# Two banks per maximum in a chain of three attention layers: pairs of banks, one bank for late projections, reciprocals by way of DRAM

## The reference

```python
# layer 0: 8 heads of 16; a bilinear position bias is added per query and per key
attn = einsum('bhdi,bhdj->bhij', q * scale, k) + pos[..., :, None] + pos[..., None, :]
y = w_proj(softmax(attn) @ v) + b_proj
out = layer_norm_over_channels(x + y)
# layers 1 and 2: 8 heads of 32
xn = group_norm(x);  q, k, v = linear(xn)
out = w_o(softmax(q k^T / sqrt(32)) v) + b_o + residual
# layer 3: a small gated attention with rank 32, without heads, at the end
```

## Time and profile before

| | |
|---|---|
| median of the timed runs | 482.24 us |
| profiled execution, its own time | 485.04 us |
| span of that execution | 483.3 us |
| TensorE busy | 453.1 us (94%), 2210 matmuls |
| VectorE busy | 362.8 us (75%) |
| ScalarE busy | 263.4 us (54%) |
| GpSimd busy | 214.4 us (44%) |
| mean granted TensorE clock | 0.968 |

### The profile page before, as it was taken

How to read it: one execution, slowest core, us unless ns; L and a number is a source line. 1 busy time by engine, 2 the same in 40 slices (tenths; PEclk the granted TensorE clock), 3 DMA queues, 4 the chain that set the end, 5 groups by cost and what they waited for, 6 DMA issues and landing times.

```text
span 483.3 us, 7009 instructions
## 1 busy us (share of the span) xinstructions
PE 453.1 (94%) x2210; PEld 239.1 (49%) x2210; DVE 362.8 (75%) x748; ACT 263.4 (54%) x515; POOL 214.4 (44%) x195
## 2 busy tenths in 40 slices
PE   8989999999896999999999799989999999979996
PEld 6544445553266575445444233657544544423463
DVE  7699888884777599987878356669997787817673
ACT  3238777775703237776757462224786677745032
POOL 8300031238010007897979811002799898960100
PEclk9979999999896999999999889999999999989999
DMA  5330544103300264679853520045388953551002
GB/s 154 56 64 21 156 69 125 22 8 62 61 6 1 60 147 100 154 155 195 189 105 57 104 48 21 1 109 126 72 176 166 191 102 70 98 100 26 0 1 87
DMA packets 20368, 41.87 MB, mean 87 GB/s; under 512 B 7170, under 2 KB 8458, under 8 KB 20076
## 3 DMA queue, kind: packets, MB, share of 16 engines
q1 hardware_dynamic: 15036, 25.41, 22.3%
q0 software_dynamic: 5152, 16.00, 17.9%
q10 hardware_dynamic: 144, 0.02, 0.0%
HBM read 5.94 MB, written 1.05 MB: 14 GB/s over the span
## 4 chain that ended last, share of the span: by engine, by line
PE 64%; DVE 10%; POOL 10%; DMA 4%; issue 4%; SPq 3%; ACT 3%; ACTq 0%; POOLq 0%; DVEq 0%
PE PV L1016 14%; PE S L977 13%; PE S L1005 13%; POOL SUMS L523 9%; DVE max L732 6%; DMA SUMS<-SUMS 3%; PE PV L929 3%; PE S L1140 3%; PE M L1029 3%; SPq L338 2%; PE PV L955 2%; PE S L1174 2%; PE M L955 2%; PE S L955 1%; SPq L331 1%
## 5 line engine op out<-in xcount | busy, mean ns | idle before, releaser
L732 DVE TENSOR_REDUCE max<-S 128x1 f32<-128x512 f32 x384 | 239.3, 683 | 39.7 <-PE S L977 38.7
L587 ACT ACTIVATE E<-S 128x512 f32<-128x512 f32 x384 | 206.5, 609 | 58.9 <-PE S L1005 53.3
L523 POOL TENSOR_TENSOR SUMS<-E 128x512 f32<-128x512 f32 x120 | 158.4, 1449 | 106.4 <-ACT E L587 102.0
L977 PE MATMUL S<-k_stack,q_stack 126*128 126x512 f32 x384 | 171.2, 460 | 5.8 <-DMA k_stack<-kL 3.4
L1005 PE MATMUL S<-q_stack,k_stack 128*128 128x512 f32 x384 | 156.0, 418 | 5.7 <-ACT E L587 5.2
L977 PEld LDWEIGHTS S<-k_stack,q_stack 126*128 126x128 f32 x384 | 72.9, 191 | 64.7 <-DVE max L732 35.4
L1005 PEld LDWEIGHTS S<-q_stack,k_stack 128*128 128x128 f32 x384 | 73.3, 193 | 38.3 <-ACT E L587 22.0
L1016 PE MATMUL PV<-E,V 128*32 128x512 f32 x768 | 92.0, 599 | 0.0
L1016 PEld LDWEIGHTS PV<-E,V 128*32 128x32 f32 x768 | 20.7, 110 | 46.9 <-issue 26.0
L498 POOL TENSOR_TENSOR att<-pv_sb,rec_sb 128x512 f32<-128x512 f32 x9 | 12.4, 1378 | 63.0 <-DMA rec_sb<-den_sb 63.0
L576 ACT ACTIVATE mHL<-S 8x128 fp32r<-8x128 f32 x48 | 12.7, 264 | 50.2 <-PE S L995 50.2
(11 more groups left out here) (175 smaller groups left out, 342.2 us busy)
## 6 DMA issues: line engine op xcount, KB each, us to landing
SUMS<-SUMS POOLq DMA_DIRECT2D x30, 512.0 KB, 5.7
k_stack<-kH SPq DMA_DIRECT2D x28, 128.0 KB, 2.3
q_stack<-qH SPq DMA_DIRECT2D x40, 64.0 KB, 2.0
rec_sb<-den_sb SPq DMA_DIRECT2D x9, 256.0 KB
q_stack<-qH SPq DMA_DIRECT2D x16, 128.0 KB, 2.8
k_stack<-kL SPq DMA_DIRECT2D x14, 128.0 KB, 4.1
k_stack<-kH SPq DMA_DIRECT2D x22, 64.0 KB, 2.3
q_stack<-qL SPq DMA_DIRECT2D x20, 64.0 KB, 2.0
```

The source lines that it names most:

```text
L523: pool.tensor_tensor(SUMS[:, slot, :], E[:, E_PLAN[s][0], :], E[:, E_PLAN[s + 1][0], :], ALU.add).then_inc(sum_ready, 1)
L587: act.activation(E[:, slot, :], B[:, ring_of_scores(s) % B_RING, :], ACT.Exp, scale=1.0 if l == 0 else float(HEAD_DIM[l]) ** -0.5).then_in ...
L732: dve.tensor_reduce(max8[:, m % 2, 2 * t + half:2 * t + half + 1], A[:, n % A_RING, :], AX.X, ALU.max).then_inc(a_used, 1)
L977: pe.matmul(A[:, n % A_RING, :], q_stack[0:SHIFT_ROW, slot, q0:q0 + P], k_stack[0:SHIFT_ROW, slot, k0:k0 + HALF], start=True, stop=True).t ...
```

## The change

- Ring A has four banks, used as two pairs. TensorE writes two banks and then signals once; VectorE takes the maxima of both in one reduce (output two elements, input 2 x 512) and signals once. TensorE waits before an even product for the pair before the last one. The seventh bank, which was M, is the fourth bank of ring A during the steps.
- Late projections all go through PV; each waits for the reader of the one directly before it. Their steps are stretched: -15 to 3 as before, then 8, 10, 14, 16, 21, 23, with new steps for ScalarE and VectorE. The second v projection of layer 0 goes through PV too.
- The denominators of blocks 0 and 1 take a slot of ring B; those of block 2 and of the last block still use M, after all maxima of the layer are read. ScalarE copies those of blocks 0 and 1 at the steps 49 and 81 in place of 54 and 86.
- The reciprocals are written to DRAM as 128 rows of 16, and spread from there to `rec_sb`.

```diff
-A_RING = 3
+A_RING = 4
-        S = ctx.enter_context(nc.psum_tensor("S", [P, 6, HALF], F32))
-        A = S[:, 0:A_RING, :]
-        B = S[:, A_RING:A_RING + B_RING, :]
-        PV = ctx.enter_context(nc.psum_tensor("PV", [P, HALF], F32))
-        M = ctx.enter_context(nc.psum_tensor("M", [P, HALF], F32))
+        banks = ctx.enter_context(nc.psum_tensor("banks", [P, 8, HALF], F32))
+        S, M, PV = banks[:, 0:6, :], banks[:, 6, :], banks[:, 7, :]
+        B = banks[:, 0:B_RING, :]
+        A = banks[:, B_RING:B_RING + A_RING, :]
...
-        LATE_PE = [{}] + 2 * [{-15 + 2 * i: (4 + i // 2, i % 2) for i in range(16)}]
-        LATE_ACT = [{}] + 2 * [{5: 8, 9: 9, 13: 10, 17: 11}]
-        LATE_DVE = [{}] + 2 * [{7: 8, 11: 9, 15: 10, 19: 11}]
+        LATE_STEPS = (-15, -13, -11, -9, -7, -5, -3, -1, 1, 3, 8, 10, 14, 16, 21, 23)
+        LATE_PE = [{}] + 2 * [{s: (4 + i // 2, i % 2) for i, s in enumerate(LATE_STEPS)}]
+        LATE_ACT = [{}] + 2 * [{5: 8, 12: 9, 18: 10, 25: 11}]
+        LATE_DVE = [{}] + 2 * [{6: 8, 13: 9, 19: 10, 26: 11}]
...
-            return (B[:, 0, :], B[:, 1, :], PV[:, :], M[:, :])[n] if n < 4 else (PV[:, :], M[:, :])[n % 2]
+            return (B[:, 0, :], B[:, 1, :], PV, M)[n] if n < 4 else PV
...
+        DENS_IN_RING = (0, BLOCKS - 2, BLOCKS - 2)
+        def ring_of_den(l, b):
+            return ring_of_scores(l, DEN_STEPS[b]) + 1
+        def den_bank(l, b):
+            return B[:, ring_of_den(l, b) % B_RING, :] if b < DENS_IN_RING[l] else M
+        rec_rows = nc.dram_tensor("rec_rows", (P, PER_ROW), F32, kind="Internal").ap()
...
                 sp.wait_ge(recs_folded, FOLDED * l + b + 1)
-                sp.dma_start(den_sb[0:P:DP, :].rearrange("u (d n) -> u d n", n=PER_ROW), rec_out[:, :]).then_inc(recs_rows, 16)
+                sp.wait_ge(recs_spread, 16 * (FOLDED * l + b))
+                sp.dma_start(rec_rows, rec_out[:, :]).then_inc(recs_rows, 16)
...
                 sp.dma_start(rec_sb[:, :],
-                             den_sb[0:P:DP, :].rearrange("u (o n) -> u o n", o=1)
+                             rec_rows.rearrange("(u o d) n -> u o (d n)", u=HEADS_B, o=1)
                              .to_broadcast([HEADS_B, DP, HALF])).then_inc(recs_spread, 16)
...
                 act.wait_ge(den_done, den_groups(l, b))
-                act.wait_ge(recs_spread, 16 * (FOLDED * l + b))
-                act.activation(den_sb[:, :], M[:, :], ACT.Copy).then_inc(den_out, 1)
+                act.wait_ge(dens_folded, 16 * (FOLDED * l + b))
+                act.activation(den_sb[:, :], den_bank(l, b), ACT.Copy).then_inc(den_out, 1)
-            DENOMINATORS_AT = [{}] + 2 * [{54: 0, 86: 1, 113: 2}]
+            DENOMINATORS_AT = [{}] + 2 * [{DEN_STEPS[0]: 0, DEN_STEPS[1]: 1, 113: 2}]
...
-                m, n = UNITS_L * l + j, STEPS * l + i
-                dve.wait_ge(a_done, n + 1)
-                if r == 0 and m >= 2:
+                m, pair = UNITS_L * l + j, (STEPS * l + i) // 2
+                dve.wait_ge(a_done, pair + 1)
+                if r == 1 and m >= 2:
                     dve.wait_ge(max_split, 3 * (m - 1))
-                t, half = maxima_tile(i)
-                dve.tensor_reduce(max8[:, m % 2, 2 * t + half:2 * t + half + 1], A[:, n % A_RING, :], AX.X,
+                (t0, half0), (t1, half1) = maxima_tile(i - 1), maxima_tile(i)
+                first, last = 2 * t0 + half0, 2 * t1 + half1
+                dve.tensor_reduce(max8[:, m % 2, first:last + 1:last - first], A[:, i % A_RING - 1:i % A_RING + 1, :], AX.X,
                                   ALU.max).then_inc(a_used, 1)
...
-                    if UNITS[l][n - 2][0] == "v":
-                        pe.wait_ge(v_out, v_count(l, n - 2))
+                    held = 2 if n == 4 else n - 1
+                    if UNITS[l][held][0] == "v":
+                        pe.wait_ge(v_out, v_count(l, held))
                     else:
-                        pe.wait_ge(split_ready, qk_count(l, n - 2))
+                        pe.wait_ge(split_ready, qk_count(l, held))
...
-                if n >= A_RING:
-                    pe.wait_ge(a_used, n - A_RING + 1)
+                pair = (STEPS * l + i) // 2
+                if i % 2 == 0 and pair >= 2:
+                    pe.wait_ge(a_used, pair - 1)
+                if i == 2:
+                    pe.wait_ge(split_ready, QK0[l] + 4)
...
-                if k == 0 and b:
-                    pe.wait_ge(den_out, den_count(l, b - 1))
+                bank, first = den_bank(l, b), HEADS_B * b
+                if k == 0 and b < DENS_IN_RING[l]:
+                    ring_free(l, ring_of_den(l, b))
+                elif k == 0:
+                    pe.wait_ge(a_used, STEPS // 2 * (l + 1))
```

61 lines of the change are left out of this document (36 added, 25 removed).

## The result

The changed kernel takes **492.81 us**, the median of 4 runs (489.44 to 494.41), against 482.51 beside it: a ratio of 1.0203, 95% interval 1.0148 to 1.0258. It is slower, by about 2%, and lies above the range given (476.5 to 487.0). The same kernel timed once more (after_again) gave 492.85 us and 1.0202 (1.0164 to 1.0241). Its profiled execution took 494.41 us with a span of 492.7, that is 9.4 more than the span of before, where the forecast had 0.7 less.

What follows compares the result with a forecast made beforehand. The pace was set by a TensorE–VectorE loop through `values`, L977 and the maxima. Layer 0 +2.4, layer 1 -2.1, layer 2 -1.0 made -0.7 us on a profiled 485.04; less 2.8 to the timed median, 481.5 us, range 476.5 to 487.0.

Steps and rivals of the forecast that it cites:

- Double maximum, 1.21 us, and idle of 1.4 to 1.6 us behind `values`: VectorE: one maximum over 1024 elements takes 1.21 us; VectorE then idles about 1.5 us a unit behind `values`.
- Steady unit 6.47 us, the loop of two pairs: Steady units: coarser handing over by pairs outweighs 0.28 us less VectorE work, 6.47 us against 6.20, +0.27 a unit.
- Layer 0 before its first `values`, "Sum 0": Layer 0's first 29 steps: -1.6 us of maxima offset by V projections through PV, pair completion and lower clock; sum 0.
- Late projections, +2.1 a layer: Layers 1 and 2 before first `values`: one bank for late projections makes step 29 later by 2.1 us, bounds -2.1 and +4.
- First `values` to ready, +1.0: Layers 1 and 2, first `values` until TensorE comes to the third denominators, before any wait: +1.0 us each.
- The stall at step 111 goes: Third denominators, layers 1 and 2: TensorE, 3.2 us late, finds the accumulate landed within 10.8 us; waits of 2.81 and 2.42 vanish.
- rival B: Stall at step 111 stays, accumulate landing later: 488.3 us, or 485 if in one layer alone; chance 0.20.
- Its gain, -5.2 and -4.1 from ready to the output projection: Layers 1 and 2, third denominators to output projection: without stall and slow denominators, 5.2 and 4.1 us shorter.
- DRAM reciprocals, "1 shorter" than 7: Spread of reciprocals from DRAM taken 1 us shorter than the 7 us from four SBUF rows; bounds 3 shorter, 2 longer.
- D (a free unit): Rival: pairs cost nothing in a steady unit (6.20 us), giving 477 us; chance 0.06.
- C (cheap late projections): Rival: late projections idle 5 us in place of 7.1, giving 477.3 us, or 473 with idle 2.9; chance 0.24.
- E: Rival: TensorE's added idle brings the lower clock into the pair stages, +4 us, giving 485 us; chance 0.10.

Runs made afterwards that it cites:

- b_late: The kernel before with only the late projections all through PV at their new steps, three single banks for maxima kept: 489.81 us, 1.0169 of the kernel before.
- a_rows: The changed kernel without its DRAM part, reciprocals spread from four SBUF rows: 497.65 us, 1.0327 of the kernel before.
- mix: The changed kernel with single maxima, three banks then four from step 43 (layer 0: 3), late projections alternating PV and M: 470.35 us, 0.9735 of the kernel before.

## Why the prediction was wrong, step by step

- **Double maximum, 1.21 us, and idle of 1.4 to 1.6 us behind `values`:** 1.22 and 1.36. Right, the idle just under its range.
- **Steady unit 6.47 us, the loop of two pairs:** 6.47, right to the hundredth. The forecast's +0.27 a unit is what nine units of layer 0 lost, 2.3 us against 2.4. The comparison that was left out is the other one, four banks one by one: against their 5.80 a pair costs 0.67 a unit.
- **Layer 0 before its first `values`, "Sum 0":** +0.65 us (52.61 against 51.96); b_late, with single maxima and the second V projection through PV, has 0.76 more too (timeline: 52.65 against 51.89), so the second projection alone can make it, and the terms that should have offset it did not. The tail of layer 0, "moves with them", took 1.3 us more: `values` at the lower clock (2.75 us against 2.16) and 0.78 us for VectorE's last sums. after_again ended its layer 0 1.1 us earlier, so part of this is one execution's.
- **Late projections, +2.1 a layer: a step that failed.** They cost 3.8 and 3.9. The forecast's +2.1 was the sum of -2.8 for VectorE's shorter work, +4.2 for idle, +0.7. In layer 1, from the first maximum to the freeing of the bank ahead of the first `values`, VectorE worked 33.7 us and stood idle 1.9 before (166.97 to 202.58); in the changed kernel it worked 31.7 and stood idle 7.6 (171.37 to 210.68). So the change was -2.0 and +5.7. The idle of 7.1 that was laid out from the rows was nearly right; the terms beside it were not. The old idle was 1.9 and not 2.9 (the old work was put at 32.8, a sum that needs 46 spacings and not the 43 it names), and the new work of 30.0 took every pair at the 1.13 us of a run, while here most pairs stand alone and take the full 1.22. Of the cost, one bank makes 2.4, more than the whole forecast, and waiting for whole pairs 1.1 or more.
- **First `values` to ready, +1.0:** +1.7 and +1.3. The units were as laid out; what came on top in layer 1 is 0.65 us for a stack DMA (244.70), which had been in time before.
- **The stall at step 111 goes:** it went, in both layers, but not for the reason given, so this part was right by luck. The forecast let TensorE's delay of 3.2 us (its own terms add up to 3.14) outlast a landing of 10.8 us or less. With that delay and the four-row spread, a_rows, the accumulate lands 11.9 us after its issue and TensorE still waits 1.60 and 1.63 us: the very wait of 1.6 that rival B had laid out for a landing of 12.2. What removed it is the spread from DRAM, beside which the same accumulate lands in 7.2 to 7.8 us. So rival B fell for the changed kernel, and its mechanism holds without the DRAM part. What the forecast took from the rule on shared engines, that the accumulates would stay crowded, fell as well; how many engines a transfer took no run shows.
- **Its gain, -5.2 and -4.1 from ready to the output projection: the other step that failed, and the largest in size (3.7 of the 10.1 us).** It was -2.6 and -3.0. after_again's layer 1, without the lower clock and without the wait for the sums, needs 19.9 us, which is what the forecast's numbers make (25.1 - 5.2 and 24.0 - 4.1). So the path was laid out rightly but for what was next late, two terms that the forecast left at nothing and gave no reason for: the lower clock in some layers (about 1.6 us, `values` of 3.51 in place of 1.92) and VectorE's last sums beside the earlier normalisation (0.8 to 1.0).
- **The base.** The gain was counted against one profiled execution in which the tail of layer 1 was 1.7 us longer than in the second one. The forecast carried the 2.8 us between that execution and the median over as a constant; part of them was in the very stretch whose gain it counted. Two executions can't say how often.
- **DRAM reciprocals, "1 shorter" than 7:** 2.2 shorter (4.9 us). The part alone is worth 5.8 us and is the only part of the change that gains when timed alone.

Of the rivals, D (a free unit) and C (cheap late projections) are refuted by rows, E by the units, which keep full clock. None of them, nor the forecast, had the late stage dearer than its row-by-row sum, though +4 stood as its upper bound: both layers at that bound would have taken 3.8 us off the miss of 11.3.

## What to carry to other kernels

In this kernel a ring between two engines was worth the number of its hand-overs and not its bytes: four banks in two pairs ran slower (6.47 us a unit) than three banks one by one (6.20), while four one by one reached 5.80. So when instructions are merged, count the hand-overs on both sides of the longest block of foreign work, and price the same banks handed over singly beside the pairs. A saving per instruction that was measured in a run of them (1.13 us a pair) is not to be had where each stands alone. When a change takes a stall away, name what is late next and what the neighbour engine will do earlier, read the tail from two profiles before its gain is entered in a sum, and ask which of two parts takes it away by leaving out one at a time.

The version that follows from this, mix with idle matmuls, runs at 468.68 us, 0.9707 (0.9677 to 0.9738) of the kernel before.

## What the runs showed of the hardware

- Half as many, twice as wide reduces from PSUM save 0.14 us each pair of banks (1.22 against 2 x 0.68), close to the 0.15 that the forecast's slope leaves of a single one (0.683 - 0.529); back to back, single ones stand 0.60 us apart, doubles 1.14, so only 0.06 of it is gained in a row of them.
- The same 256 KB broadcast to 128 partitions lands 2.2 us earlier from DRAM than from four SBUF rows (4.9 and 7.1 us), and an accumulating DMA in flight beside it lands sooner too: unit 11's takes 7.2 to 7.8 us beside the DRAM spread and 10.7 to 12.2 beside the four-row one.
- VectorE's sum of two SBUF tiles takes 0.69 us, and 1.58 to 1.77 when GpSimd's multiplication began ahead of it; when the sum began first it kept its 0.69, and the multiplication took up to 1.8 in place of 1.28.
- The lower clock is not bound to the longest wait. It was there at once behind the six waits of 1.9 to 2.8 us at the third denominators (the kernel before twice, b_late) and behind one of a_rows' two waits of 1.6 us. Without such a wait, 6 of 20 layers had it behind three waits of 0.3 to 0.5 us, and the two profiles of the changed kernel had it in different layers.
